# Differential attention on one core: another order of its products, a ring of four result banks, and the causal mask as one 128x128 product per head

## What is computed

```python
q = qkv[..., :2 * Hx].reshape(Bx, 2 * NQ, Sx, HD)
k = qkv[..., 2 * Hx:2 * Hx + G].reshape(Bx, NKV, Sx, HD)
v = qkv[..., 2 * Hx + G:].reshape(Bx, NKV, Sx, HD)
...
scores = jnp.einsum('bhqd,bhkd->bhqk', q, k) / math.sqrt(HD)
scores = jnp.where(causal, scores, -jnp.inf)
aw = jax.nn.softmax(scores, axis=-1)
...
aw = aw[:, :, 0] - lam * aw[:, :, 1]
attn = jnp.einsum('bhqk,bhkd->bhqd', aw, v) * (1.0 - LAMBDA_INIT)
```

## Time and profile before

| | us |
|---|---|
| median of three runs | 6575.94 (6566.96 to 6585.18) |
| the profiled execution | 6587.06 |
| its span, first to last instruction | 6585.4 |
| the L2 attention's unit loops in it (2534.45 to 2893.55 and 2923.10 to 3277.80) | 713.8 |
| of these, 26 full slots, from one turning of maxima to the next | 557.3 |

### The profile page before, as it was taken

The page is one execution under the profiler, slowest core; times in us unless marked ns, Lnnn a source line. Parts: engine busy times, 40 slices in busy tenths (PEclk is TensorE's granted clock), DMA queues, the critical chain, the costliest instruction groups (busy, mean ns, idle before and its releaser), DMA issues. The chain is left out here.

```text
span 6585.4 us, 104299 instructions
## 1 busy us (share of the span) xinstructions
PE 5021.5 (76%) x40177; PEld 3326.4 (51%) x40177; DVE 3368.4 (51%) x7604; ACT 2376.2 (36%) x4640; POOL 2237.6 (34%) x2170
## 2 busy tenths in 40 slices
PE   5988987349999878999978888888888881002776
PEld 3666664225555434444456666666666660001555
DVE  2011112541222014333277878888887876786665
ACT  1011010112111223233356666666666661001665
POOL 1000000010000001101188888888888870003653
PEclk8565565569988986566599999999999995556998
DMA  0000000000000000000021211111111110001000
GB/s 15 0 1 1 0 1 4 0 14 1 1 1 1 18 0 4 1 1 1 1 72 39 55 39 55 39 55 39 55 39 38 39 34 2 0 0 31 19 19 17
DMA packets 96027, 123.69 MB, mean 19 GB/s; under 512 B 33305, under 2 KB 50050, under 8 KB 94802
## 3 DMA queue, kind: packets, MB, share of 16 engines
q1 hardware_dynamic: 95570, 117.24, 6.7%
HBM read 29.63 MB, written 1.05 MB: 5 GB/s over the span
## 5 line engine op out<-in xcount | busy, mean ns | idle before, releaser
L398 POOL TENSOR_TENSOR t_inv<-t_ssq,half 128x8 f32<-128x8 f32 x448 | 778.0, 1738 | 157.3 <-DVE t_ssq L657 146.6
L449 PE MATMUL t_wa<-t_w_qkv,t_resid 128*128 128x512 f32 x1344 | 662.0, 619 | 39.3 <-DMA t_b<-in_L_ffn_b 36.4
L409 POOL TENSOR_TENSOR t_ra<-t_qn,t_rot 128x512 f32<-128x512 f32 x448 | 569.0, 1270 | 85.0 <-DVE t_qn L664 77.0
L596 ACT ACTIVATE t_p<-t_p 128x384 f32<-128x384 f32 (+1 forms) x448 | 241.3, 539 | 540.3 <-DVE t_p L681 531.0
L2227 PE MATMUL a_bank<-ident,a_gate 128*128 128x128 f32 x16 | 4.5, 433 | 505.0 <-POOL a_gate L2218 505.0
L690 DVE TENSOR_TENSOR t_ra<-t_ra,t_rb 128x512 f32<-128x512 f32 x448 | 322.2, 743 | 111.5 <-POOL t_rb L411 110.4
L1867 PE MATMUL a_B<-a_Q,a_K 9*128 9x256 f32 (+3 forms) x1024 | 371.5, 677 | 4.1 <-ACT a_pt L1921 4.1
L449 PEld LDWEIGHTS t_wa<-t_w_qkv,t_resid 128*128 128x128 f32 x1344 | 231.7, 193 | 265.3 <-issue 235.5
L1921 ACT ACTIVATE a_pt<-a_B 128x512 f32<-128x512 f32 (+1 forms) x384 | 183.7, 525 | 502.1 <-PE a_B L1867 501.6
L1081 DVE RECIPROCAL a_rden<-a_all 128x24 f32<-128x24 f32 x16 | 4.9, 308 | 699.3 <-PE a_all L1024 699.3
L1943 DVE TENSOR_REDUCE a_nmax<-a_A 128x2 f32<-128x256 f32 (+3 forms) x256 | 207.2, 824 | 301.3 <-PE a_A L1856 300.0
(11 more groups left out here) (412 smaller groups left out, 11686.8 us busy)
## 6 DMA issues: line engine op xcount, KB each, us to landing
t_v<-t_vn SPq DMA_DIRECT2D x192, 198.0 KB, 2.6
t_v<-t_vn SPq DMA_DIRECT2D x248, 132.0 KB, 2.4
t_v<-t_vn SPq DMA_DIRECT2D x144, 66.0 KB, 2.0
t_w_qkv<-in_L_ffn_Wqkv SPq DMA_DIRECT2D x6, 1536.0 KB
t_v<-t_nothing SPq DMA_DIRECT2D x48, 66.0 KB, 2.0
t_w_o<-in_L_ffn_Wo SPq DMA_DIRECT2D x6, 512.0 KB
f_h<-t_L_ffn_h_w SPq DMA_DIRECT2D x2, 1024.0 KB, 8.1
t_w<-in_L_ffn_W SPq DMA_DIRECT2D x6, 341.0 KB
```

The source lines that it names most:

```text
L398: pool.tensor_tensor(inv[:, n % 2, r, :], ssq[:, n % 2, r, :], g["half"][:, 0:8], ALU.pow).then_inc(inved.sem, 1)
L409: pool.tensor_tensor(ra[:, n % 2, r], qn[:, r], spread(cos, 1, 8), ALU.mult).then_inc(cosd.sem, 1)
L449: pe.matmul(bank, resid[:, b, lo:lo + P], w_qkv[:, l % 2, at:at + 512], start=True, stop=True).then_inc(wa_up.sem, 1)
```

## The change

The order of a slot is new. For h = 0 to 5 two chunks come first, then the score; h = 6 and 7 have the score alone. The turning of maxima and the weighing both stand behind score 3, the output behind score 5. Chunks take the heads in the order 2, 3, 0, 1 (`part_of`), scores take the query tiles from the last to the first (`tile_of`), so the 512-column scores come first. The bank `O` joins the ring `B`, which has four banks, and the weighing claims a bank of it like the others. The mask of a score is one product of the whole 128x128 mask with the 128x128 identity for each head, so two products of 128 rows and 128 columns a score, in the place of 8 of 32 rows and 32 columns. VectorE's and ScalarE's programs follow the same order. A constant array is added that nothing here reads.

```diff
-        cmask = st.sb("cmask", [P, 4, P], BF16)
+        cmask = st.sb("cmask", [P, P], BF16)
...
-        B = st.bank("B", [P, 3, 512])
-        O = st.bank("O", [P, 512])
+        B = st.bank("B", [P, 4, 512])
...
-                sp.dma_start(cmask[:, :, :], d["c_cmask"]).then_inc(loaded, 16)
+                sp.dma_start(cmask[:, :], d["c_causal"][0]).then_inc(loaded, 16)
...
             for u in range(-2, UNITS + 1):
                 for h in range(8):
+                    if 0 <= u < UNITS and h < 6:
+                        order += [("chunk", u, 2 * h), ("chunk", u, 2 * h + 1)]
                     if u + 2 < UNITS:
                         order.append(("score", u + 2, h))
-                    if 0 <= u < UNITS:
-                        for c in range(3 * h // 2, 3 * (h + 1) // 2):
-                            order.append(("chunk", u, c))
-                    if h == 1 and 0 <= u + 1 < UNITS:
+                    if h == 3 and 0 <= u + 1 < UNITS:
                         order.append(("maxima", u + 1, 0))
-                    if h == 2 and 0 <= u - 1 < UNITS:
+                    if h == 3 and 0 <= u - 1 < UNITS:
                         order.append(("weigh", u - 1, 0))
-                    if h == 6 and 0 <= u - 1 < UNITS:
+                    if h == 5 and 0 <= u - 1 < UNITS:
                         order.append(("out", u - 1, 0))
             for kind, u, c in order:
-                if kind in ("chunk", "maxima", "out"):
+                if kind != "score":
                     job_of[kind, u, c] = len(jobs)
                     jobs.append((kind, u, c))
+            part_of = lambda c: (c // 4, (2, 3, 0, 1)[c % 4])
+            tile_of = lambda h: (TPB - 1 - h // 2, h % 2)
...
-                        if k >= 3:
-                            was, m, i = jobs[k - 3]
+                        if k >= 4:
+                            was, m, i = jobs[k - 4]
...
+                            elif was == "weigh":
+                                pe.wait_ge(o_in.sem, o_in.at(m))
...
-                        t, pair = divmod(h, 2)
-                        if u or t:
-                            pe.wait_ge(maxed.sem, maxed.at(u, h - 1) if t else maxed.at(u - 1, 7 + pair))
+                        t, pair = tile_of(h)
+                        if u or h >= 2:
+                            pe.wait_ge(maxed.sem, maxed.at(u, h - 1) if h >= 2 else maxed.at(u - 1, 7 + pair))
                         heads = (2 * pair, 2 * pair + 1)
-                        for i in range(4):
-                            for j in heads:
-                                rows = slice(32 * j, 32 * j + 32)
-                                at = t * P + 32 * i
-                                pe.matmul(A[:, j, at:at + 32], cmask[rows, i, :], identb[rows, rows], start=(i == 0), stop=False, skip_group_check=True)
+                        for j in heads:
+                            pe.matmul(A[:, j, t * P:(t + 1) * P], identb[:, :], cmask[:, :], start=True, stop=False, skip_group_check=True)
...
-                        k, j = divmod(c, GH)
+                        k, j = part_of(c)
...
-                        if u:
-                            pe.wait_ge(o_in.sem, o_in.at(u - 1))
                         pe.wait_ge(exped.sem, exped.at(u, 12))
+                        bank = claim("weigh", u, 0)
...
-                                m = pe.matmul(O[32 * j:32 * j + 32, kt * P:SEQ], va[:, kv, kt, b0 + bl, :],
+                                m = pe.matmul(bank[32 * j:32 * j + 32, kt * P:SEQ], va[:, kv, kt, b0 + bl, :],
...
-                            if c == 6 and u:
-                                act.wait_ge(weighed.sem, weighed.at(u - 1))
+                            if c == 7 and u:
+                                b = job_of["weigh", u - 1, 0]
+                                act.wait_ge(B_up.sem, b + 1)
...
-                                act.activation(oS[:, (u - 1) % 2, :], O[:, :], ACT.Copy).then_inc(o_in.sem, 1)
+                                act.activation(oS[:, (u - 1) % 2, :], B[:, b % 4, :], ACT.Copy).then_inc(o_in.sem, 1)
...
-                            if h == 1 and 0 <= u + 1 < UNITS:
+                            if h == 3 and 0 <= u + 1 < UNITS:
                                 shift(u + 1)
-                            if h == 6 and 0 <= u - 1 < UNITS:
+                            if h == 5 and 0 <= u - 1 < UNITS:
                                 finish(u - 1)
```

More of the change, by code:

```diff
@@ L1659, in attention2 @@
         A = st.bank("A", [P, 4, 512])
-        B = st.bank("B", [P, 3, 512])
-        O = st.bank("O", [P, 512])
-        banks = [A[:, i, :] for i in range(4)] + [B[:, i, :] for i in range(3)] + [O[:, :]]
+        B = st.bank("B", [P, 4, 512])
+        banks = [A[:, i, :] for i in range(4)] + [B[:, i, :] for i in range(4)]
         loaded = st.sem("loaded")
@@ L1821, in attention2 @@
             selected = st.event("selected" + hn, 4)
-            weighed = st.event("weighed" + hn)
             o_in = st.event("o_in" + hn)
@@ L1838, in claim @@
                                 pe.wait_ge(shifted.sem, shifted.at(m))
+                            elif was == "weigh":
+                                pe.wait_ge(o_in.sem, o_in.at(m))
                             else:
                                 pe.wait_ge(normed.sem, normed.at(m))
-                        return B[:, k % 3, :]
+                        return B[:, k % 4, :]
                     def score(u, h):
-                        t, pair = divmod(h, 2)
-                        if u or t:
-                            pe.wait_ge(maxed.sem, maxed.at(u, h - 1) if t else maxed.at(u - 1, 7 + pair))
+                        t, pair = tile_of(h)
+                        if u or h >= 2:
+                            pe.wait_ge(maxed.sem, maxed.at(u, h - 1) if h >= 2 else maxed.at(u - 1, 7 + pair))
                         heads = (2 * pair, 2 * pair + 1)
-                        for i in range(4):
-                            for j in heads:
-                                rows = slice(32 * j, 32 * j + 32)
-                                at = t * P + 32 * i
-                                pe.matmul(A[:, j, at:at + 32], cmask[rows, i, :], identb[rows, rows], start=(i == 0), stop=False, skip_group_check=True)
+                        for j in heads:
+                            pe.matmul(A[:, j, t * P:(t + 1) * P], identb[:, :], cmask[:, :], start=True, stop=False, skip_group_check=True)
                         for j in heads:
@@ L1885, in weigh @@
                             for j in range(GH):
-                                m = pe.matmul(O[32 * j:32 * j + 32, kt * P:SEQ], va[:, kv, kt, b0 + bl, :],
+                                m = pe.matmul(bank[32 * j:32 * j + 32, kt * P:SEQ], va[:, kv, kt, b0 + bl, :],
                                               pt[:, u % 2, j, START[kt]:START[kt] + (TPB - kt) * P], start=(kt == 0), stop=(kt == TPB - 1),
                                               tile_position=(0, 32 * j), skip_group_check=True)
-                        m.then_inc(weighed.sem, 1)
+                        m.then_inc(B_up.sem, 1)
                     def turn_out(u):
@@ L1918, in _ @@
                                 if c == 0 and u >= 2:
-                                    act.wait_ge(weighed.sem, weighed.at(u - 2))
+                                    act.wait_ge(B_up.sem, job_of["weigh", u - 2, 0] + 1)
                                 at = sum(WIDTH[:k])
-                                act.activation(pt[:, u % 2, j, at:at + WIDTH[k]], B[:, b % 3, 0:WIDTH[k]], ACT.Exp).then_inc(exped.sem, 1)
-                            if c == 6 and u:
-                                act.wait_ge(weighed.sem, weighed.at(u - 1))
+                                act.activation(pt[:, u % 2, j, at:at + WIDTH[k]], B[:, b % 4, 0:WIDTH[k]], ACT.Exp).then_inc(exped.sem, 1)
+                            if c == 7 and u:
+                                b = job_of["weigh", u - 1, 0]
+                                act.wait_ge(B_up.sem, b + 1)
                                 if u >= 3:
                                     act.wait_ge(normed.sem, normed.at(u - 3))
-                                act.activation(oS[:, (u - 1) % 2, :], O[:, :], ACT.Copy).then_inc(o_in.sem, 1)
+                                act.activation(oS[:, (u - 1) % 2, :], B[:, b % 4, :], ACT.Copy).then_inc(o_in.sem, 1)
                 @block.gpsimd
@@ L1949, in shift @@
                         row = Q[:, u].rearrange("p t r -> p (t r)")
-                        v.tensor_tensor(row, B[:, b % 3, :], row, ALU.add).then_inc(shifted.sem, 1)
+                        v.tensor_tensor(row, B[:, b % 4, :], row, ALU.add).then_inc(shifted.sem, 1)
                     def finish(u):
@@ L1955, in finish @@
                         v.wait_ge(B_up.sem, b + 1)
-                        out = B[:, b % 3, :].rearrange("p (t j e) -> p t j e", t=TPB, e=32)
+                        out = B[:, b % 4, :].rearrange("p (t j e) -> p t j e", t=TPB, e=32)
```

(1 more changed line is left out.)

## The result

The changed kernel takes 6685.1 us (median of four runs, 6674.28 to 6692.46), and stands to the kernel before, measured with it (6575.4), as 1.0165, with a 95% interval of 1.0145 to 1.0185. It is slower by about 109 us. The profiled execution took 6692.46 us, its span 6690.8.

What follows compares the result with a forecast made beforehand. TensorE was taken as the bound: gated slots of 29.7 us at half clock, 25.4 with full stretches, against 21.4. The loops' +104, +15, +8 and -10 sum to +117 us, giving 6693 us, range 6630 to 6770.

Steps and rivals of the forecast that it cites:

- The gate: Before every score: all row groups empty, masks run, all start again, leaving only one pair of groups with work.
- its first rival: At the masks: products slide in between working row groups, the order runs as laid out, about 6410 us; chance 4%.
- The sum of a slot: Full slot: scores 9.7, chunks 9.4, masks 4.0, rest 6.6, so 29.7 us at half clock, 25.4 after clock gain.
- The pair of masks with its gates: Ahead of each score: two masks and both gates cost 0.5 us, range 0.4 to 0.7; eight make 4.0 us.
- the rival in which the weights are waited for in full: At the masks: products on new rows wait for their weights, a pair costs 0.9 us, about 6780 us; chance 10%.
- the step of 0.15: In scores and chunks: 0.15 us between a product's two records, 1.2 us for scores and 0.9 for chunks a slot.
- The clock: Behind maxima and weighing: at least one full-clock stretch a slot, gaining 4.3 us for 2.7, bounds 2.7 and 6.
- The rival in which the clock pays the loss back: Over the full slots: longer whole-array work holds full clock, no change or faster, 6537 us with two more stretches; chance 5%.
- The slots' +104: 26 full slots: each goes from 21.4 to 25.4 us, adding 104 us.
- The small terms: Outside full slots: unit 0's two slots +15 us, four scores-only slots +8, last slots without scores -10.
- the upper bound of a slot, 27.8: Full slot: forecast 25.4 us with bounds 23.7 and 27.8; masks at 0.7 a pair would add 1.6.
- The ring: Four-bank ring and the weighing's claim on it: costed at nothing, since the banks' earlier work is done in time.

Runs made afterwards that it cites:

- the gate-only run: Changed kernel, its masks replaced by one 128-row, single-column product per head ahead of each score: 6651.5 us, ratio 1.0093 to the kernel before.
- the run with four gates: Changed kernel, its 16 full-height mask products a slot gathered four at a time, ahead of both scores of a tile: 6456.0 us, ratio 0.9806.
- small masks: Changed kernel, new order and four-bank ring kept, each score masked by 8 products of 32 rows and 32 columns as before: 6394.0 us, ratio 0.9703.
- the row masks: Changed kernel, each mask as four products of 32 rows and 128 columns in its own head's row group: 6435.7 us, ratio 0.9783.

## Why the prediction was right

The forecast was 6693 us, in a range of 6630 to 6770; the measured time is 6685.1 us.

**Bound.** TensorE set the time and still does; it is busy for all of 307.8 and 299.3 us.

**The gate.** The prediction takes each mask as a gate, and its first rival is that there is none. The trace has the gate at every mask that can be read; the gate-only run and the run with four gates show that it, and not the mask's work, makes most of the time. The rival's 6410 us came close to the same order with small masks: 6394 us, 15.3 us a slot where it had 15.0.

**The sum of a slot.** Forecast 25.4 us, measured 25.3. Scaled to half clock, the measured slots are 25.65 x 0.58 / 0.50 = 29.8 and 24.94 x 0.60 / 0.50 = 29.9 us, against 29.7 in the sum. The terms: with the masks at 0.5 a pair my terms for the piece from the output to the next turned maxima make 18.2 us at half clock, and 17.75 is measured. The pair of masks with its gates I had at 0.50: it is 0.14 ahead (the chunks from 2606.74 have two records of 0.85 us of columns each, the second right behind the first, so they end near 2608.45; the mask starts at 2608.59) and 0.32 from there to the score, 0.46 together, between the 0.43 of the earlier trace rows and the 0.55 of the earlier trace rows and far from the 0.9 of the rival in which the weights are waited for in full. Mask to mask are 4.04 us, reckoned 0.50 + 1.86 + 1.86 = 4.2; the step of 0.15 between a chunk's two records, which I had charged, isn't there in these chunks. I take it that their weights were loaded while the score ran, which no run shows. (The prediction writes 2 x 0.22 as 0.43, which is 0.44; it counts with 0.427, and that agrees with the 0.43 between the starts of two records of 256 columns that it reads in the earlier trace rows.)

**The clock.** I took 4.3 us a slot of gain from full clock. 0.58 and 0.60 over the slots mean 16 and 20% of their time at full clock (0.5 is none, 1.0 all of it), so 0.16 x 25.65 = 4.1 and 0.20 x 24.94 = 5.0 us of a slot at full speed, in which twice the work is done, so that as much time is saved. In the slot shown, a full stretch begins while the weighing ends and holds over the next two pieces (1.00, 1.00); before, the slot at the head of the earlier trace rows had none. A full stretch stands in 21 of the 26 full slots before and in all 24 after, so it came more surely, as reckoned; that the turned maxima and the weighing in one piece are the reason is argued and not shown. The rival in which the clock pays the loss back did not come: 0.56 and 0.58 before became 0.58 and 0.60 only.

**The loops.** The slots' +104 is right: (25.3 - 21.4) x 26 = +101. The small terms, +15, +8 and -10, were to add 13; both loops together went from 713.8 us to 407.5 + 406.0 = 813.5 (2534.17 to 2941.71 and 2972.50 to 3378.50), so 99.7 in all, and the small terms made nothing together. The terms can be told apart if the loops are cut at the first chunks of the slots 0, 1 and 14. The last piece, the slots without scores, before (two halves) and after:

```profile
2854.22:2893.55 39.33, 34.05 (x179) 14.64 (x175) 4.63 (x14) 13.35 (x29) 5.61 (x9) 0.63 0.00 1
3236.08:3277.80 41.72, 36.01 (x180) 16.16 (x175) 4.64 (x14) 13.45 (x29) 5.61 (x9) 0.54 0.00 1
2912.71:2941.71 29.00, 25.80 (x182) 13.68 (x182) 4.64 (x17) 12.62 (x27) 5.00 (x8) 0.76 0.01 1
3347.24:3378.50 31.26, 27.97 (x181) 14.83 (x181) 4.20 (x15) 12.52 (x27) 5.00 (x8) 0.66 0.00 1
```

The 26 slots gained 101.0 us (556.3 to 657.3), the two slots of unit 0 14.0 (33.5 to 47.5) and the scores-only slots 5.5 (43.0 to 48.5). The last slots lost 20.8 us (81.05 to 60.26), twice the forecast's 10. This is a slip in the prediction's sum: its own figures, 12 us before less 7.2 after, are 5 us a slot, and a half has two such slots, so 10 a half and 20 in all. Likewise its scores-only slots, 13.7 against 12.3 and 14.8 against 13.2, are 1.4 and 1.6 more and not 2 each, and the upper bound of a slot, 27.8, is neither 29.7 - 2.7 = 27.0 nor 28.6 with masks at 0.7 a pair. With the two slips mended the forecast would be some 12 us lower. The span grew by 105.4 us in all, so 5.7 us lie outside the loops, where only the load of the mask was changed; the changed kernel's four runs differ by 18 us among themselves.

**The ring.** Costed at nothing, and rightly so in this kernel: behind gates three or four banks make no difference to a path with two groups at work. The trace bears that out as far as it goes: in the first half's full slots TensorE waits for another engine only ahead of masks, for VectorE's maxima (20.3 us of idle weight loading, 15 times), and never for a bank. No run has the new order and the gates with the old ring, but order and ring together bring only 0.1 points where the gates are (1.0179 to 1.0165), within the noise. Once the gates are gone, the ring is worth 0.8 points.

A better version came out of it. New order, ring of four and no mask at all on the scores is 3.6% faster than the kernel before. The 0.6 points beyond the small masks go with the larger share of full clock, by the estimate at the row masks. The mask there serves only to keep the future keys out of the row's maximum, and that maximum is a shift that cancels between numerator and sum; the triangle itself is zeroed by GpSimd behind the exponential. A larger shift is as good as long as the exponentials stay well above the smallest numbers, which depends on the size of the scores; where that isn't sure, the small masks keep 3.0%.

## What to carry to other kernels

Where small products run side by side in row groups, a product over the full height was a barrier in this kernel, with 128 columns and with one: put it into the row groups, even at four times the columns, or gather such products behind one barrier. Two edits that each look like a saving (fewer mask products, an order for four groups) have to be costed together, by drawing what stands between two barriers and which row groups have work there. Busy time does not show the loss (TensorE was busy throughout in the version with gates and in that without): count the records that overlap, or the columns per microsecond.

## What was not expected of the hardware

Products do not all start in the order of the program. In the kernel before, chunks 10 and 11 stand between score 7 and score 0 of the next slot (the first order listing above). Its trace has score 0 first:

```profile
2701.35 0.29 PE L1853 MATMUL a_A<-identb,a_cmask 32*128 32x32 bf16 x8
2701.48 0.77 PE L1856 MATMUL a_A<-a_K,a_Q 9*128 9x128 f32 x4
2702.05 1.18 PE L1867 MATMUL a_B<-a_Q,a_K 9*128 9x512 f32 x1
2702.33 1.06 PE L1856 MATMUL a_A<-a_K,a_Q 9*128 9x512 f32 x2
```

Score 0, on groups 0 and 1, starts at 2701.48, and chunk 0 of 512 columns at 2702.05, while score 7 holds groups 2 and 3, its second records from 2702.33, and chunks 10 and 11, which stand ahead of score 0 in the program, have not begun; their four records start at 2703.18 and 2703.61. The Trainium skill ("TensorE: Matmul & The Clock Gate", Part 3) has products start strictly in program order; this trace shows it otherwise across row groups. That this is what lets a loosely ordered stream fill four groups, and what a full-height product takes away, is my reading; no run isolates it.

The granted clock stayed at 0.50 with TensorE busy throughout in the changed kernel too (17.75 of 17.75 us in one piece), while the run without masks had 0.72 over its slots, with no idle TensorE either (157.57 of 157.57 us). Eleven slots of it, and eleven of the run with the gate alone:

```profile
2585.07:2742.64 157.57, 157.57 (x1146) 95.65 (x1145) 86.74 (x143) 66.66 (x144) 27.39 (x44) 0.72 0.00 1
2603.59:2872.18 268.59, 268.59 (x1323) 137.01 (x1321) 89.19 (x143) 68.69 (x143) 27.39 (x46) 0.58 0.00 1
```

So part of what the gates cost is the share of full clock. An estimate from these two rows: scaled to half clock a slot is 24.4 x 0.58 / 0.50 = 28.3 us with the gates and 20.6 without. At a clock of 0.72 the 28.3 would be 19.7 us. Of the 10.1 us between 14.3 and 24.4, 5.4 are then lost overlap and 4.7 the lower clock. In the changed kernel and in the one without masks a full stretch begins in every full slot while the weighing ends or just behind it. How the clock would go with all of the slot's work on the full height, no run here shows.
